# Reordering the stretch behind the rounds, and splitting GpSimd's two gathers around its sum

## The chip, the core and the metric

The kernel runs on one core of one Trainium2 chip. The metric is device time of that core in microseconds (us). Engines are named as the profile names them: PE (TensorE, matrix products), ACT (ScalarE), DVE (VectorE), POOL (GpSimd), SP (SyncE, here only a queue that starts DMAs). Each engine runs its own list of instructions in order; they wait for one another by semaphores.

## What is computed

16384 tokens (rows of 512 numbers) pass through a layer norm, then two branches whose product is added to the input. One branch is a circular filter in the Fourier domain followed by a small error-correcting code; the other is a mixture of 8 experts, of which each token uses two.

```
xn = _layernorm(x, axis=-1)
# branch s
x1  = ifft(fft(xn) * filt).real
bits = (sigmoid(x1 @ W_el + b_el) > 0.5)
s = x1 + golay_correct(bits) @ W_le + b_le
# branch g
logits = xn @ router_w.T
probs = softmax(logits); topk_vals, topk_idx = top_k(probs, 2)
expert_out = einsum('nh,eho->eno', xn, expert_weights)
g = silu(sum over the two experts of (expert_out + prob) * weight)
x = x + s * g
```

## The kernel before

Four stages follow one another. Times are from the profiled execution.

**Rounds (0 to 233 us).** Eight rounds of 16 tiles of 128 tokens each read all tokens, compute logits and bits, and store a 32-number information row per token in DRAM (`token_info`). Every token gets a slot in a table sorted by its pair of experts (`pair_tokens`).

**The stretch behind the rounds (233 to 283 us).** Two things happen side by side. First, the table is turned into a list of tiles: DVE computes where the last round's tokens go, and makes 16 pairs of marks (L1208, L1209) that PE multiplies (L1459); DVE copies the product (L1225); PE multiplies it and two loaded rows with a selection matrix (L1465); DVE writes the token list `tile_tok` (L1227); ACT copies its columns to `gidx` (L727); POOL gathers by them (L560 token rows `x2`, L562 information rows `inf2`). Second, the experts' weights are split into two fp16 parts: `high` on ACT (L646 sum half, L647 difference half) writes the high part `w_hi`; the low part `w_lo` of the first `ON_PE` = 4 experts in `EXPERT_ORDER` is made by PE, four chunks each (L1450, L1451), and evicted by ACT (L710); that of the other four by DVE in the next stage (`low_sums` L966, `low_differences` L973, each 128x1024, at the steps in `LOW_AT`).

**Extra tiles (283 to 373 us).** 27 tiles (n = 1 to 27; tile 0 is a placeholder) that hold tokens of two neighbouring pairs, one expert each. For tile n: gather (POOL), `halves_of` (DVE, L1264 to L1268), `high_part` (ACT, L733), `low_part` (DVE, L1274), a turn by eight PE transposes (L1492), its copy (ACT, L758), twelve matmuls (PE, L1481 to L1483), scaling (ACT, L775), adding (DVE, L1286). `extra_step(n)` on PE turns tile n+1 before it multiplies tile n; on DVE it does `halves_of(n+4)`, `low_part(n+3)`, the addition of n, and then the expert work of `LOW_AT`.

**Main tiles (373 to 1208 us).** 128 tiles, in loops over four. For each tile PE does 24 expert matmuls (L1481 to L1483) and 13 of the filter (L1523 to L1531). POOL adds the input (`step`, L582: sg2 + x2), then gathers tile m+4 into the same buffers (L560, L562), then scatters the finished tile (L566). `gidx` for tile m+4 is copied by ACT as the last act of its own step m (L727). A tile's buffers are taken as landed when both gathers have counted on the one semaphore `ld_x2[k]`. SP turns a tile by a DMA transpose (L459) once DVE's split and ACT's bits are there.

The order of the work on each engine is the order in which it is written; no scheduler moves it.

## Time and profile before

| | us |
|---|---|
| median of three runs | 1216.6 (1215.72 to 1217.47) |
| the profiled execution, its own time | 1215.48 |
| its span, first to last instruction | 1213.6 |
| rounds | 233 |
| stretch behind the rounds | 50.4 |
| extra tiles, 27 | 90 |
| main tiles, 128 | 835 |

The stage borders are read from the first expert matmul (283.43) and the last of the extra tiles (about 373). A line of the timeline gives start, duration, engine, line and operation, then in brackets how long the engine sat idle before it and what released it.

### The profile page before, as it was taken

The page shows a single profiled execution, that of the slowest core. Times are in us where ns is not written, and L with a number is a line of the kernel's source. Part 1 is how long each engine was busy: PE and PEld are TensorE (multiplying, and loading weights), DVE is VectorE, ACT ScalarE, POOL GpSimd, SP SyncE. Part 2 cuts the span into 40 slices and gives each one's busy share as a digit, 9 for nine tenths or more (in the row PEclk, how much of TensorE's full clock was granted, in tenths as well). Part 3 has the DMA queues.
Part 4 walks back from the last instruction along what each step waited for, and adds up shares of the span by engine and source line. Part 5 has one row for each costly group of instructions (what it writes and reads, how often), then busy time and mean ns, then how long its engine had stood idle before and what let it go on. Part 6 is the DMA issues. An engine that isn't in the chain of part 4 may idle for free. (4 is left out here: it accounts for less than half of the span.)

```text
span 1213.6 us, 27062 instructions
## 1 busy us (share of the span) xinstructions
PE 1138.5 (94%) x6310; PEld 613.3 (51%) x6311; DVE 1039.4 (86%) x2368; ACT 641.5 (53%) x1531; POOL 811.2 (67%) x715
## 2 busy tenths in 40 slices
PE   5999898667999999999999999999999999999996
PEld 4555555333454455554555555555555555555553
DVE  6799999977886889899888888888888888888874
ACT  4466656466784434434555545554555455555543
POOL 1226656846783777777777777777777777777774
PEclk9999999878999999999999999999999999999998
DMA  8656756013555776667455455555545554554552
GB/s 324 228 202 219 222 177 182 18 34 103 166 170 150 169 173 172 158 177 164 120 129 137 121 127 138 128 129 129 136 122 132 133 127 130 129 132 125 130 134 76
DMA packets 205774, 178.17 MB, mean 147 GB/s; under 512 B 164671, under 2 KB 171247, under 8 KB 201634
## 3 DMA queue, kind: packets, MB, share of 16 engines
q1 hardware_dynamic: 170258, 98.61, 32.1%
q0 software_dynamic: 31248, 76.95, 21.7%
q10 hardware_dynamic: 4224, 2.10, 0.6%
q8 instruction: 19, 0.31, 0.1%
q14 instruction: 25, 0.20, 0.0%
HBM read 94.83 MB, written 45.02 MB: 115 GB/s over the span
## 5 line engine op out<-in xcount | busy, mean ns | idle before, releaser
L1481 PE MATMUL banks<-w_hi,arena 128*128 (+1 forms) x1076 | 409.1, 380 | 6.0 <-DMA arena<-arena 4.3
L1483 PE MATMUL banks<-w_hi,arena 128*128 (+1 forms) x1076 | 408.7, 380 | 0.0
L1482 PE MATMUL banks<-w_lo,arena 128*128 (+1 forms) x1076 | 408.7, 380 | 0.0
L560 POOL DMA_INDIRECT xbuf<-in_L_attn_x,gidx x155 | 175.9, 1135 | 139.9 <-POOL xbuf L582 88.8
L733 ACT ACTIVATE arena<-xbuf,inf 128x512 f16<-128x512 f32 x141 | 101.8, 722 | 279.8 <-DVE xbuf L1268 279.8
L562 POOL DMA_INDIRECT inf<-token_info,gidx x155 | 192.9, 1245 | 52.3 <-issue 51.0
L582 POOL TENSOR_TENSOR xbuf<-xbuf 128x512 f32<-128x512 f32 x128 | 167.2, 1306 | 39.8 <-DVE xbuf L1325 34.3
L1264 DVE TENSOR_TENSOR xbuf<-xbuf 128x256 f32<-128x256 f32 x155 | 148.4, 957 | 50.8 <-DMA inf<-token_info,gidx 43.9
L531 POOL DMA_INDIRECT pair_tokens<-tok,slot x112 | 110.9, 990 | 98.1 <-DVE slot L1107 65.8
L1481 PEld LDWEIGHTS banks<-w_hi,arena 128*128 128x128 f16 x1076 | 105.3, 98 | 128.6 <-issue 16.6
L566 POOL DMA_INDIRECT out<-xbuf,sidx x128 | 142.7, 1115 | 41.3 <-issue 40.7
L1483 PEld LDWEIGHTS banks<-w_hi,arena 128*128 128x128 f16 x1076 | 105.4, 98 | 124.6 <-issue 1.0
L1482 PEld LDWEIGHTS banks<-w_lo,arena 128*128 128x128 f16 x1076 | 105.3, 98 | 111.9 <-issue 0.8
L1308 DVE SCALAR_TENSOR_TENSOR arena<-banks,cab,xT 128x512 f32<-128x512 f32 x128 | 95.9, 749 | 31.9 <-PE banks L1483 28.3
L1402 PE MATMUL banks<-xT,wcat 128*128 128x512 f32 x256 | 120.6, 616 | 0.8 <-issue 0.4
L1274 DVE SCALAR_TENSOR_TENSOR arena<-xbuf,inf,arena 128x512 f16<-128x512 f32 x141 | 105.8, 750 | 11.7 <-ACT arena L733 8.1
L1325 DVE TENSOR_TENSOR xbuf<-xbuf,arena 128x512 f32<-128x512 f32 x128 | 88.7, 693 | 17.4 <-DVE xbuf L1319 0.5
L1319 DVE TENSOR_TENSOR xbuf<-xbuf 128x256 f32<-128x256 f32 x256 | 97.4, 422 | 4.4
L752 ACT ACTIVATE cab<-inf,unscale 128x1 f32 x256 | 73.9, 288 | 42.9 <-issue 42.1
L789 ACT ACTIVATE xbuf<-banks 128x384 f32<-128x384 f32 x128 | 62.3, 487 | 63.9 <-PE banks L1531 63.7
L1265 DVE TENSOR_TENSOR xbuf<-xbuf 128x256 f32<-128x256 f32 x155 | 95.4, 615 | 0.0
L793 ACT ACTIVATE arena<-arena,inf 128x512 f32<-128x512 f32 x128 | 91.1, 712 | 2.7 <-DVE arena L1308 2.7
(322 smaller groups left out, 1877.2 us busy)
## 6 DMA issues: line engine op xcount, KB each, us to landing
xbuf<-in_L_attn_x SPq DMA_DIRECT2D x32, 1024.0 KB, 6.0
arena<-in_L_ffn_expert_weights SPq DMA_DIRECT2D x8, 1024.0 KB, 9.6
arena<-extra_sums SPq DMA_DIRECT2D x30, 256.0 KB, 2.7
extra_sums<-arena SPq DMA_DIRECT2D x28, 256.0 KB, 2.5
xbuf<-in_L_attn_x,gidx POOLq DMA_INDIRECT x155
inf<-token_info,gidx POOLq DMA_INDIRECT x155
token_info<-info ACTq DMA_DIRECT2D x8, 256.0 KB, 5.9
arena<-arena SPq DMA_TRANSPOSE x128
```

Source lines behind the costliest of these rows:

```text
L531: pool.indirect_dma_start(out=pair_slots, out_offset=bass.IndirectOffsetOnAxis(ap=slot[:, buf, t:t + 1], axis=0), in_=tok[:, buf, t:t + 1] ...
L560: pool.indirect_dma_start(out=x2[:, k], out_offset=None, in_=x_rows, in_offset=tokens, bounds_check=N - 1, oob_is_err=False).then_inc(ld_x ...
L562: pool.indirect_dma_start(out=inf2[:, k], out_offset=None, in_=info_dram, in_offset=tokens, bounds_check=N - 1, oob_is_err=False).then_inc ...
L566: pool.indirect_dma_start(out=out_rows, out_offset=bass.IndirectOffsetOnAxis(ap=sidx[:, k:k + 1], axis=0), in_=o2[:, k % 2], in_offset=Non ...
L582: G.tensor_tensor(o2[:, b], sg2[:, b], x2[:, k], ALU.add).then_inc(o_ready, 1)
L733: nc.scalar.activation(hi4[ring(i, k)], uv2[:, b], ACT.Copy, scale=inf2[:, k, 1:2]).then_inc(hi_ready, 1)
L1264: V.tensor_tensor(raw2[:, b, 0:H], x2[:, k, 0:H], x2[:, k, H:E], ALU.add).then_inc(raw_ready, 1)
L1274: V.scalar_tensor_tensor(lo4[ring(i, k)], uv2[:, b], inf2[:, k, 1:2], hi4[ring(i, k)], ALU.mult, ALU.subtract).then_inc(split_ready, 1)
L1402: last = mm(psum[:, 2], wcat[:, c], xT4[:, k % 2, c], start=(c == 0), stop=(c == C - 1))
L1481: mm(ps, hi[:, c], wh, start=(c == 0), stop=False)
L1482: mm(ps, hi[:, c], wl, start=False, stop=False)
L1483: end = mm(ps, lo[:, c], wh, start=False, stop=(c == C - 1))
```

## The change

**The low parts.** `ON_PE` goes from 4 to 3: the fourth expert's low part goes from PE and ACT to DVE. Its sum half stands in front of DVE's wait for the token list, its difference half and the fifth expert's sum half in front of the first `halves_of`. The remaining halves are spread by `SUMS_AT` and `DIFFERENCES_AT` over steps 1, 2, 3, 13 and 19, where `LOW_AT` had both halves together at 1, 2, 3 and 12.

**ACT's order.** `high` is cut in halves, and one eviction (`low_chunk`) stands before each of eight of them. Two evictions of the third expert's low part come ahead of `gidx`, two behind.

**PE's order.** Two chunks of the third expert stand between the marks and the selection product, two behind it.

**DVE's order.** Eleven small operations that stood behind the 16 pairs of marks are put among the first six pairs (`tile_places`).

**POOL's step.** In the main tiles the information row's gather for tile m+4 comes ahead of the sum of tile m, behind new waits for `gidx_ready` and `g_ready` (ACT has read the buffer's last value for tile m), and the token rows' gather stays behind the sum.

```diff
-    LOW_AT = {1: 4, 2: 5, 3: 6, 12: 7}
-    ON_PE = 4
+    ON_PE = 3
+    SUMS_AT = {2: 5, 3: 6, 13: 7}
+    DIFFERENCES_AT = {1: 4, 2: 5, 3: 6, 19: 7}
...
+                if not last:
+                    pool.wait_ge(gidx_ready, j + U + 1)
+                    pool.wait_ge(g_ready, m + 1)
+                    pool.sem_inc(g_seen, 1)
+                    gather_info(k)
                 pool.wait_ge(sg_ready, m + 1)
...
-                if not last:
-                    pool.wait_ge(gidx_ready, j + U + 1)
                 pool.wait_ge(o_ready, m + 1)
                 pool.sem_inc(o_seen, 1)
                 if not last:
-                    gather(k)
+                    gather_rows(k)
                 scatter_out(k)
...
-            for n in range(3):
-                high(EXPERT_ORDER[n])
-            low(0)
-            high(EXPERT_ORDER[3])
-            low(1)
-            for n in range(4, NE - 1):
-                high(EXPERT_ORDER[n])
+            high(EXPERT_ORDER[0])
+            high(EXPERT_ORDER[1])
+            for n in range(2):
                 for c in range(C):
+                    low_chunk(n, c)
+                    high_half(EXPERT_ORDER[2 + 2 * n + c // 2], c % 2)
+            high(EXPERT_ORDER[6])
+            low_chunk(2, 0)
+            low_chunk(2, 1)
...
-            low(2)
-            low(3)
             high(EXPERT_ORDER[NE - 1])
+            low_chunk(2, 2)
+            low_chunk(2, 3)
...
             V.tensor_copy(tokTl, psum[:, 0, 0:P]).then_inc(rows_float, 1)
+            low_sums(3)
             dve.wait_ge(toks_mm, 1)
...
             dve.sem_inc(split_ready, 1)
+            low_differences(3)
+            low_sums(4)
             halves_of(0, 1)
...
-                if n in LOW_AT:
-                    low_parts(LOW_AT[n])
+                if n in SUMS_AT:
+                    low_sums(SUMS_AT[n])
+                if n in DIFFERENCES_AT:
+                    low_differences(DIFFERENCES_AT[n])
...
             last.then_inc(last_mm, 1)
-
+            low(2, (0, 1))
...
-            low(2)
-            low(3)
+            low(2, (2, 3))
```

PE in the stretch behind the rounds, before: the marks' product, the selection product, then all of the third expert (the fourth, eight more such rows, follows it). `arena` and `w_lo` hold the weights' halves, `latT` the rows that are selected.

```order
L1459 MATMUL banks<-arena 128x128 [waits last_marks] x16
L1465 MATMUL banks<-latT 128x156 [waits rows_float]
L1465 MATMUL banks<-latT 128x156 x2
L1450 MATMUL banks<-w_lo,arena 128x512 [waits low_out,scaled_ready,whi_ready]
L1451 MATMUL banks<-w_hi,minus_h 128x512
L1450 MATMUL banks<-w_lo,arena 128x512 [waits low_out]
```

PE at the same place, after:

```order
L1493 MATMUL banks<-arena 128x128 [waits last_marks] x16
L1484 MATMUL banks<-w_lo,arena 128x512 [waits low_out,scaled_ready,whi_ready]
L1485 MATMUL banks<-w_hi,minus_h 128x512
L1484 MATMUL banks<-w_lo,arena 128x512 [waits low_out]
L1485 MATMUL banks<-w_hi,minus_h 128x512
L1499 MATMUL banks<-latT 128x156 [waits rows_float]
L1499 MATMUL banks<-latT 128x156 x2
```

Two chunks, four rows, have moved ahead of the selection product.

ACT at the end of the same stretch, before: the token indices, then eight evictions, then the last expert's high part, then the first extra tile.

```order
L727 ACTIVATE gidx<-tile_tok 128x1 [waits tiles_ready]
L727 ACTIVATE gidx<-tile_tok 128x1 x3
L710 ACTIVATE w_lo<-banks 128x512 [waits low_mm] x8
L646 ACTIVATE w_hi<-w_lo,wscale 128x1024
L647 ACTIVATE w_hi<-arena,wscale 128x1024
L733 ACTIVATE arena<-xbuf,inf 128x512 [waits uv_ready,live_ready,pad_ready]
```

ACT at the same place, after:

```order
L727 ACTIVATE w_lo<-banks 128x512 [waits low_mm] x2
L746 ACTIVATE gidx<-tile_tok 128x1 [waits tiles_ready]
L746 ACTIVATE gidx<-tile_tok 128x1 x3
L660 ACTIVATE w_hi<-w_lo,wscale 128x1024
L662 ACTIVATE w_hi<-arena,wscale 128x1024
L727 ACTIVATE w_lo<-banks 128x512 [waits low_mm] x2
L752 ACTIVATE arena<-xbuf,inf 128x512 [waits uv_ready,live_ready,pad_ready]
```

Six of the eight evictions behind the indices are gone from there: two stand ahead of them, four (the fourth expert's) are no longer made.

POOL in one main step of the loop, before: the sum, the two gathers, the scatter.

```order
L581 ISA [waits sg_ready]
L582 TENSOR_TENSOR xbuf<-xbuf 128x512 [waits stored0]
L585 REGISTER_ALU [waits sidx_ready]
L560 DMA xbuf<-in_L_attn_x,gidx 128x512 [waits gidx_ready,o_ready]
L562 DMA inf<-token_info,gidx 128x32
L566 DMA out<-xbuf,sidx 16384x512
```

POOL in the same step, after:

```order
L591 REGISTER_ALU [waits gidx_ready]
L568 DMA inf<-token_info,gidx 128x32 [waits g_ready]
L596 ISA [waits sg_ready]
L597 TENSOR_TENSOR xbuf<-xbuf 128x512 [waits stored0]
L562 DMA xbuf<-in_L_attn_x,gidx 128x512 [waits sidx_ready,o_ready]
L572 DMA out<-xbuf,sidx 16384x512
```

The information gather and the wait for `gidx_ready` have moved ahead of the sum; a wait for `g_ready` is new.

## Rows read from the trace of the kernel before

**Rows 1.** Timeline (start, us, operation) of PE's weight loads: first filter matmul, neighbouring main tiles.

```profile
1002.42 0.10 PEld L1523 LDWEIGHTS banks<-wle,arena 96*128 96x128 bf16 x1
...
1008.81 0.10 PEld L1523 LDWEIGHTS banks<-wle,arena 96*128 96x128 bf16 x1
```

**Rows 2.** The same instruction by line: count, ns min/median/max, first and last start.

```profile
L1523 PE MATMUL banks<-wle,arena x128: 381/381/382, 380.3 to 1202.0; 96*128 96x512 bf16 x128
```

**Rows 3.** Timeline of PE among the extra tiles: turns that waited (idle before, releaser).

```profile
304.16 0.62 PE L1492 MATMUL banks<-ident_h,xT 128*128 128x128 f16 x8 [1.77 <-DVE xT L1274]
333.46 0.62 PE L1492 MATMUL banks<-ident_h,arena 128*128 128x128 f16 x8 [1.75 <-DVE arena L1274]
```

**Rows 4.** Timeline of PE, stretch behind the rounds.

```profile
264.56 1.93 PE L1465 MATMUL banks<-latT 128*128 128x156 f32 x6 [2.15 <-DVE latT L1225]
266.28 1.91 PE L1450 MATMUL banks<-w_lo,arena 128*128 128x512 f32 x2
...
275.88 1.02 PE L1450 MATMUL banks<-arena 128*128 128x512 f32 x2
...
283.43 0.61 PE L1481 MATMUL banks<-w_hi,arena 128*128 128x512 f16 x1 [0.22 <-ACT arena L758]
```

**Rows 5.** Timeline of POOL, the same stretch: token rows of tiles 1 and 2.

```profile
268.30 1.02 POOL L560 DMA_INDIRECT xbuf<-in_L_attn_x,gidx  x1 [10.57 <-ACT gidx L727]
...
270.92 1.00 POOL L560 DMA_INDIRECT xbuf<-in_L_attn_x,gidx  x1 [0.30 <-issue]
```

**Rows 6.** Timeline of DVE, the same stretch.

```profile
262.02 0.19 DVE L1211 TENSOR_REDUCE spots<-tq 128x1 f32<-128x28 f32 x1
...
263.88 0.42 DVE L1223 TENSOR_TENSOR latT<-tokT,latT 128x256 f32<-128x256 int32 x1
...
266.52 0.32 DVE L1227 TENSOR_SCALAR tile_tok<-banks 128x156 int32<-128x156 f32 x1 [2.02 <-PE banks L1465]
...
272.33 0.43 DVE L1264 TENSOR_TENSOR xbuf<-xbuf 128x256 f32<-128x256 f32 x1 [3.02 <-DMA inf<-token_info,gidx]
...
280.47 0.75 DVE L1274 SCALAR_TENSOR_TENSOR arena<-xbuf,inf,arena 128x512 f16<-128x512 f32 x1 [1.88 <-ACT arena L733]
```

**Rows 7.** Timeline of ACT, the same stretch.

```profile
267.18 0.47 ACT L727 ACTIVATE gidx<-tile_tok 128x1 int32<-128x1 int32 x4
...
277.65 1.14 ACT L646 ACTIVATE w_hi<-w_lo,wscale 128x1024 f16<-128x1024 f32 x1
...
279.73 0.71 ACT L733 ACTIVATE arena<-xbuf,inf 128x512 f16<-128x512 f32 x1
```

**Rows 8.** Timeline of DVE among the extra tiles: one half of an expert's low part.

```profile
294.72 1.28 DVE L966 SCALAR_TENSOR_TENSOR w_lo<-w_lo,wscale,w_hi 128x1024 f16<-128x1024 f32 x1
```

**Rows 9.** The page's groups of POOL: busy us, mean ns of one, idle before.

```profile
L560 POOL DMA_INDIRECT xbuf<-in_L_attn_x,gidx x155 | 175.9, 1135 | 139.9 <-POOL xbuf L582 88.8
...
L562 POOL DMA_INDIRECT inf<-token_info,gidx x155 | 192.9, 1245 | 52.3 <-issue 51.0
L582 POOL TENSOR_TENSOR xbuf<-xbuf 128x512 f32<-128x512 f32 x128 | 167.2, 1306 | 39.8 <-DVE xbuf L1325 34.3
...
L566 POOL DMA_INDIRECT out<-xbuf,sidx x128 | 142.7, 1115 | 41.3 <-issue 40.7
```

**Rows 10.** Timeline of POOL over a main tile's sum and the next gather.

```profile
704.03 1.27 POOL L582 TENSOR_TENSOR xbuf<-xbuf 128x512 f32<-128x512 f32 x1
706.17 1.13 POOL L560 DMA_INDIRECT xbuf<-in_L_attn_x,gidx  x1 [0.87 <-POOL xbuf L582]
```

**Rows 11.** Timeline of DVE over the same main tile.

```profile
703.24 0.69 DVE L1325 TENSOR_TENSOR xbuf<-xbuf,arena 128x512 f32<-128x512 f32 x1
704.12 1.48 DVE L1264 TENSOR_TENSOR xbuf<-xbuf 128x256 f32<-128x256 f32 x1 [0.19 <-DMA inf<-token_info,gidx]
```

**Rows 12.** Timeline of ACT over the same main tile.

```profile
703.31 0.18 ACT L727 ACTIVATE gidx<-tile_tok 128x1 int32 x1
...
707.68 0.49 ACT L789 ACTIVATE xbuf<-banks 128x384 f32<-128x384 f32 x1 [0.44 <-PE banks L1531]
```

More of the change, by code:

```diff
@@ L322, in build @@
         o_seen = sem("o_seen")
+        g_seen = sem("g_seen")
         last_marks, last_mm = sems("last_marks last_mm")
@@ L554, in _, with gather_rows @@
                 pool.wait_ge(info_stored[b], 16 * (R // 2))
-            def gather(k):
+            def gather_rows(k):
                 tokens = bass.IndirectOffsetOnAxis(ap=gidx[:, k:k + 1], axis=0)
@@ L568, in scatter_out, with gather @@
                                         bounds_check=N - 1, oob_is_err=False).then_inc(stored[k % 2], 16)
+            def gather(k):
+                gather_rows(k)
+                gather_info(k)
             def extra_gather(n):
@@ L588, in step @@
                 if not last:
-                    gather(k)
+                    gather_rows(k)
                 scatter_out(k)
@@ L642, in _, with high_half @@
             norm(1)
+            def high_half(e, part):
+                if part == 0:
+                    nc.scalar.activation(w_hi[:, e, 0:CH], quart[:, e], ACT.Copy, scale=wscale[:, e, 1:2])
+                else:
+                    nc.scalar.activation(w_hi[:, e, CH:C], diff[:, DIFF_AT[e]], ACT.Copy, scale=wscale[:, e, 0:1]).then_inc(whi_ready, 1)
             def high(e):
-                nc.scalar.activation(w_hi[:, e, 0:CH], quart[:, e], ACT.Copy, scale=wscale[:, e, 1:2])
-                nc.scalar.activation(w_hi[:, e, CH:C], diff[:, DIFF_AT[e]], ACT.Copy, scale=wscale[:, e, 0:1]).then_inc(whi_ready, 1)
+                high_half(e, 0)
+                high_half(e, 1)
             def latT_copy(i, k):
@@ L704, in _, with low_chunk @@
             act.wait_ge(wsc_ready, 1)
-            def low(n):
-                e = EXPERT_ORDER[n]
-                for c in range(C):
-                    act.wait_ge(low_mm, C * n + c + 1)
-                    nc.scalar.activation(w_lo[:, e, c], psum[:, LOW_BANKS[c]], ACT.Copy).then_inc(low_out, 1)
-            for n in range(3):
-                high(EXPERT_ORDER[n])
-            low(0)
-            high(EXPERT_ORDER[3])
-            low(1)
-            for n in range(4, NE - 1):
-                high(EXPERT_ORDER[n])
+            def low_chunk(n, c):
+                act.wait_ge(low_mm, C * n + c + 1)
+                nc.scalar.activation(w_lo[:, EXPERT_ORDER[n], c], psum[:, LOW_BANKS[c]], ACT.Copy).then_inc(low_out, 1)
+            high(EXPERT_ORDER[0])
+            high(EXPERT_ORDER[1])
+            for n in range(2):
+                for c in range(C):
+                    low_chunk(n, c)
[3 more added lines that the diff above has]
+            low_chunk(2, 1)
             def bits_part(i, k):
@@ L974, in low_differences @@
                                        ALU.subtract).then_inc(wlo_ready, 1)
-            def low_parts(n):
-                low_sums(n)
-                low_differences(n)
             def stat(i, k, q):
@@ L1206, in _, with note, tile_places @@
             link(V.scalar_tensor_tensor(tokTf[:, 1], iota_c, tsel[:, 1, 1:2], tokTf[:, 1], ALU.is_ge, ALU.mult))
+            def note(ins):
+                n[0] += 1
+                ins.then_inc(dch, 1)
+            def tile_places(t):
+                if 0 < t < 6:
+                    dve.wait_ge(dch, n[0])
+                if t == 0:
+                    V.tensor_reduce(upto_n, up_to, AXX, ALU.add)
+                    V.tensor_reduce(shared, to_tile[:, 0, 0:NX], AXX, ALU.max)
+                    note(V.tensor_tensor_scan(home, carry_c[:, 1:NQ * TB:TB], opens, -1.0, ALU.mult, ALU.add))
+                if t == 1:
+                    V.tensor_tensor(homes, home, own_c, ALU.mult)
+                    note(V.scalar_tensor_tensor(apart, lane_c, 1.0, home[:, NQ - 1:NQ], ALU.add, ALU.add))
+                if t == 2:
+                    V.tensor_reduce(own_home, homes, AXX, ALU.add)
+                    note(V.tensor_tensor(apart, apart, upto_n, ALU.subtract))
+                if t == 3:
+                    note(V.scalar_tensor_tensor(gap, upto_n, 1.0, apart, ALU.subtract, ALU.subtract))
+                if t == 4:
+                    V.tensor_scalar(to_tile[:, 1, NX:NT], iota_c, own_home, None, ALU.is_equal)
+                    note(V.scalar_tensor_tensor(spot, gap, shared, apart, ALU.mult, ALU.add))
+                if t == 5:
+                    V.tensor_scalar(to_tile[:, 0, NX:NT], iota_c, spot, None, ALU.is_equal)
             for t in range(TB):
@@ L1210, in _ @@
                                 ALU.mult).then_inc(last_marks, 1)
[L1211 to L1221 removed]
+                tile_places(t)
             dve.wait_ge(rows_loaded, 32)
@@ L1440, in _, with low @@
             rank(R - 1)
-            def low(n):
+            def low(n, chunks=range(C)):
                 e = EXPERT_ORDER[n]
@@ L1446, in low @@
                 pe.wait_ge(scaled_ready, 2 * n + 2)
-                for c in range(C):
+                for c in chunks:
                     after(pe, low_out, C * (n - 1) + c + 1)
```

14 lines of the change are left out of this document (3 added, 11 removed).

## The prediction

> **What bounds the kernel now.** I read PE's pace in the main tiles first, then the turns that waited among the extra tiles, then the timelines of all engines in the stretch behind the rounds.
>
> The main tiles are set by PE. Where nothing waits, a tile's first filter matmul stands 6.39 us behind that of the tile before [rows 1]; over all 128 tiles the mean is (1202.0 - 380.3) / 127 = 6.47 [rows 2]. All that PE loses there is 0.08 x 127 = 10 us of 822, and no edit of the main step can give back more. The extra tiles are near PE's pace too, but for three turns that waited 1.75 to 1.77 us each for DVE's split; the last two are in [rows 3], the first lies five microseconds ahead of them. In the stretch behind the rounds PE has done its last weight chunk at 277 and starts the first extra tile at 283.43 [rows 4]. That is a chain over all engines, and there time is to be had.
>
> What ends that chain? Tile 1's rows are requested at 268.30 [rows 5] and DVE halves them from 272.33 [rows 6] to about 273.6. But ACT converts them only at 279.73, straight behind the last expert's high part that began at 277.65 [rows 7]: it had eight evictions to get through, paced by PE's low parts of two experts. Not the gather is late, but ACT's queue.
>
> **Part 1, the start of the extra tiles.** Four evictions and one expert on PE are gone, two more evictions are ahead of the indices. Behind the indices ACT has the last high part (2.1 us, 277.65 to 279.73, [rows 7]) and two evictions (together one us, half as wide as a conversion of 1.04). Even with indices at 270 it is free by 273.7, before tile 1 is halved. So the gather is late next. From the first request G (268.30 before): tile 2's rows are requested 2.62 later [rows 5]; a tile's halves start 4.03 behind its request (268.30 to 272.33, [rows 5, 6]), tile 2's at G + 6.65. They count because DVE halves tiles 1 and 2 before it splits tile 1. They take 1.2, so the split starts at G + 7.85. From there to the first expert matmul it is 283.43 - 280.47 = 2.96 [rows 4, 6]. The first extra tile starts at G + 10.8. With G unchanged: 279.1, a gain of 4.3.
>
> **Part 2, what moves G.** DVE's small operations took 1.86 us (262.02 to 263.88, [rows 6]), in part waiting for each other. Among the marks they cost about 1.2 (an estimate from these rows: a third of the time is links). PE's selection product could start half a microsecond earlier than 264.56 [rows 4], if PE were free. It isn't: two chunks now stand ahead of it. A chunk's two fp32 matmuls took 1.91 us at 266.28, at the half clock, and 1.02 at 275.88, at the full one [rows 4]; with the third matmul two chunks are 4.2 or 2.15. They start behind the last mark, at about 263.6.
> - At the full clock the chunks end at 265.8 and the product (1.2 instead of 1.93) at 267.0. ACT reached the indices at 267.18, straight from a conversion [rows 7], and now has two evictions more ahead of them, so the indices come at 268.2, 1.0 later.
> - At the half clock the chunks end at 267.8, the product at 269.7, and the indices come at 270.1, 2.9 later.
>
> PE's rate came back while it worked without a break between these two rows, and the chunks give it such work earlier. I take the middle: chunks until 267.4, the product at the full rate, indices at 269.2, 2.0 later. G is then 270.3, the first extra tile starts at 281.1, a gain of **2.3 us**, with ends of 1.4 and 3.3. POOL has two scalings fewer and waits for the indices in every case (10.57 us before, [rows 5]): nothing.
>
> DVE has new work there, three halves of 1.28 us [rows 8]. The first lies in its wait for the selection product (2.02, [rows 6], longer now), the other two in the wait for tile 1's rows (3.02, [rows 6]): nothing, at worst 0.5.
>
> **Part 3, low parts among the extra tiles.** Before, DVE has eight halves of 1.28 there [rows 8], two each in steps 1, 2, 3 and 12. Now it has seven: one in step 1, two each in 2 and 3, one in 13 and one in 19. The two waits near 299 and 304 (3.5 together) follow steps 1 to 3. One half less takes up to 1.28 off, but DVE's first addition comes some 0.4 later against PE's start than before, as DVE waits for tile 2; I take 0.8. The wait at 333.46 (1.75, [rows 3]) follows two halves in one step; with one half it should lose 1.28, less a little for step 19. I take 1.2. Sum: **2.0 us**, ends 0.8 and, with all three waits gone, 5.3.
>
> **Part 4, POOL's main step.** POOL works nearly as long per tile as PE: 1.14 + 1.25 + 1.31 + 1.12 [rows 9], a gap of 0.87 [rows 10] and two of 0.3 make 6.3 us against 6.39 to 6.47. The reorder leaves this sum and adds a wait and a count. What does it do to the landing? Before, the information rows are requested last, 1.43 behind the token rows (1.13 and 0.3). Now the token rows are last and nothing comes between sum and request. Against that the sum is later. The product is ready at 703.24 + 0.69 = 703.93 [rows 11], and the sum followed at 704.03 [rows 10]. The indices that the gather needs are written at 703.49 [rows 12] and it takes 1.0 to 1.3, so the sum starts at about 704.85, 0.8 later. And the token rows (256 KB against 16) take some 0.7 longer to land, an estimate from the 4.03 for both and the 1.3 between their requests. So 1.43 earlier, 0.8 and 0.7 later: about zero. What the later sum touches has little room: ACT idles 0.44 before its next eviction [rows 12], DVE 0.19 before its halves [rows 11]. Queued behind the new wait on POOL are the sum, the scatter and tile m+4's token rows. I take **0**, ends of 3 us each way: of the 10 us that PE loses, the waits for transposed tiles are the part that a landing could change.
>
> DVE's first halving takes 1.48 us beside POOL's sum [rows 11], and 0.43 where POOL sums nothing [rows 6]. The Trainium skill (SBUF — State Buffer, Who interferes with whom) says that a DVE instruction with two SBUF inputs and a GpSimd instruction that reads SBUF exclude each other, for the whole of the one that came first. By this rule the later sum blocks one of the next three operations for as long, and nothing is won; by the row alone one could hope for 1 us of DVE time per tile, which isn't late anyway. The sum of the terms is the same by both.
>
> **Sum.** 2.3 + 2.0 + 0 = 4.3 us. The profiled execution took 1215.48; with 4.3 off it is 1211.2. It lies 1.1 below the median of 1216.6, so the median comes to **1212.3 us**.
>
> **Rivals.** First, the start barely moves and the turns go on waiting: PE stays at the half clock and the indices come 2.9 later (1.4 gained), DVE gives 0.8, the main tiles cost 0.5. 1214.9, no change. For it: pairs of 1.91 us at this very place. Against: ACT's queue falls away in any case.
>
> Second, POOL's step becomes the pace of the main tiles. A circle closes over two tiles: indices of tile m, gather (1.3), sum (1.3), gap (0.9), landing of the token rows (3.4, from 4.03 less 0.6), halves beside the sum (2.3), ACT's conversion, eviction, activation, bits, two coefficients and the next indices (about 3.5). That is 12.7 us, and PE does two tiles in 12.8 to 12.9. It decides once the circle grows by 0.2. At 0.1 us per tile beyond PE's pace it costs 12 us in 120 tiles: 1216.6 - 4.3 + 12 = 1224. For it: DVE already waited for the information rows [rows 11], and the later sum uses up what room there is. Against: POOL's own work is no longer.
>
> Third, the landing is earlier and helps: PE's waits in the main tiles fall by 3, and all three turns among the extra tiles are in time (5.3). With 2.3 at the start that is 10.6, 1206.0.
>
> Fourth, the edits of the stretch don't do what they say: DVE's three halves delay tile 1, or the indices wait for ACT, and the first matmul stays at 283. Part 3 alone is left: 1214.6, no change.
>
> **Chances.** Forecast 0.52 (1209 to 1214); first and fourth together 0.2; second 0.13; third 0.15. The range of 8 in 10 runs from 1206.0 to 1218.0: the third case to the first and fourth with the worst end of Part 4; it leaves out most of the second. What a measurement of this kernel can tell from no change is about 0.2%, 2.4 us; faster means below 1214.2. From the cases: faster 0.67, same 0.2, slower 0.13.
>
> **What would show it.** The first expert matmul at 281 (279.8 to 282.2) instead of 283.43, with ACT idle before tile 1's conversion and DVE waiting for tile 2's rows: Part 1. The index copy at about 269, behind the selection product and not behind ACT's conversions: Part 2; the time of the two chunks shows the clock. Shorter waits of the turns and none near step 12: Part 3. The filter's matmuls 6.47 apart on average: Part 4; 6.5 or more is the second rival, with POOL never idle or waiting for the indices. The forecast is wrong if the first matmul comes earlier but the end of the extra tiles does not, or if the spacing moves either way by more than 0.03.

## The result and the profile after

The changed kernel takes 1281.49 us, median of four runs (1278.05 to 1284.93), against 1216.16 for the kernel before, run beside it (four runs, 1214.67 to 1217.47). The ratio is 1.0538, 95% interval 1.0512 to 1.0563: 65 us slower, where 4 us faster was forecast. The span of the profiled execution is 1279.0.

**Where the time went.** The filter's first matmul by line, the instruction of [rows 2] (count, ns, first and last start):

```profile
L1556 PE MATMUL banks<-wle,arena x128: 381/381/382, 378.8 to 1267.8; 96*128 96x512 bf16 x128
```

Up to the first main tile the changed kernel is 1.5 us ahead (378.8 against 380.3). Then a tile takes (1267.8 - 378.8) / 127 = 7.00 us instead of 6.47; this mean distance is called the spacing in what follows. That is 0.53 x 127 = 67 us: the whole loss lies in the main tiles. It runs through all of them, but not evenly. By PE's weight load for this matmul, the first 32 tiles take 7.25 us each (378.62 to 610.60; before 6.57), the other 95 take 6.92 (before 6.44).

**Who is waited for.** The page's groups of after, columns as in [rows 9]:

```profile
L1514 PE MATMUL banks<-w_hi,arena 128*128 (+1 forms) x1076 | 411.5, 382 | 57.4 <-DMA arena<-arena 53.9
...
L752 ACT ACTIVATE arena<-xbuf,inf 128x512 f16<-128x512 f32 x141 | 101.8, 722 | 447.5 <-DVE xbuf L1298 447.5
L568 POOL DMA_INDIRECT inf<-token_info,gidx x155 | 172.8, 1115 | 165.4 <-ACT gidx L746 82.4
L562 POOL DMA_INDIRECT xbuf<-in_L_attn_x,gidx x155 | 171.2, 1105 | 144.2 <-issue 125.5
...
L1294 DVE TENSOR_TENSOR xbuf<-xbuf 128x256 f32<-128x256 f32 x155 | 137.2, 885 | 55.7 <-DMA xbuf<-in_L_attn_x,gidx 38.3
```

Every engine waits: PE for the transposed tile, ACT for DVE's halves, DVE for the token rows, and POOL, ahead of its information gather, for ACT's indices. None is busy all the time: POOL's busy time even fell to 786.2 us (811.2 before). Each waits for the next one, and the last for the first. That is a closed chain: a circle of waits in which no single engine's load sets the pace.

**The closed chain, followed once round.** Timelines of the changed kernel over two main tiles (start, duration, engine, line; idle before in brackets). In POOL's step for tile m the rows of tile m+4 are requested; DVE and ACT halve and convert them in their step m+2, where ACT also copies the index of tile m+6, and POOL's step m+2 waits for that index. So one round of the circle spans two tiles. POOL:

```profile
702.87 1.01 POOL L562 DMA_INDIRECT xbuf<-in_L_attn_x,gidx  x1 [0.87 <-issue]
...
706.11 1.02 POOL L568 DMA_INDIRECT inf<-token_info,gidx  x1 [0.90 <-ACT gidx L746]
707.16 1.27 POOL L597 TENSOR_TENSOR xbuf<-xbuf 128x512 f32<-128x512 f32 x1
709.30 1.11 POOL L562 DMA_INDIRECT xbuf<-in_L_attn_x,gidx  x1 [0.87 <-issue]
...
713.33 1.18 POOL L568 DMA_INDIRECT inf<-token_info,gidx  x1 [1.17 <-DVE xbuf L1355]
714.54 1.27 POOL L597 TENSOR_TENSOR xbuf<-xbuf 128x512 f32<-128x512 f32 x1
716.68 1.02 POOL L562 DMA_INDIRECT xbuf<-in_L_attn_x,gidx  x1 [0.87 <-issue]
```

DVE and ACT in the same stretch:

```profile
705.23 0.69 DVE L1355 TENSOR_TENSOR xbuf<-xbuf,arena 128x512 f32<-128x512 f32 x1
706.48 2.24 DVE L1294 TENSOR_TENSOR xbuf<-xbuf 128x256 f32<-128x256 f32 x1 [0.56 <-DMA xbuf<-in_L_attn_x,gidx]
...
709.24 0.28 DVE L1298 TENSOR_TENSOR xbuf<-xbuf 128x128 f32<-128x128 f32 x1
```

```profile
705.00 0.18 ACT L746 ACTIVATE gidx<-tile_tok 128x1 int32 x1
...
709.64 0.72 ACT L752 ACTIVATE arena<-xbuf,inf 128x512 f16<-128x512 f32 x1 [3.46 <-DVE xbuf L1298]
...
710.64 0.71 ACT L812 ACTIVATE arena<-arena,inf 128x512 f32<-128x512 f32 x1
...
712.20 0.20 ACT L746 ACTIVATE gidx<-tile_tok 128x1 int32 x1
```

Token rows are requested at 702.87 and halved from 706.48 (3.61). The halves end at 709.52 and ACT converts at 709.64 (3.16). ACT's eviction, activation, bits, coefficients and index copies end at 712.40 (2.76). The information gather starts at 713.33 (0.93), the sum at 714.54 (1.21), and the token rows two tiles further on are requested at 716.68 (2.14). Together that is 13.81 us for two tiles, 6.91 a tile, and PE's own pace is 6.39 [rows 1].

The profile puts POOL's wait at 713.33 down to DVE's line 1355, the product, which had ended at 713.28. But the gather has no wait for the product, only for the index and for ACT's activation (`gidx_ready`, `g_ready`). At 706.11 it stands 0.93 behind the index copy's end (705.18), and at 713.33 again 0.93 (712.40). It was the index both times, and not in these two tiles alone: between 600 and 1150 us the gather starts 0.91 to 0.99 behind the end of an index copy in 78 of 80 tiles. DVE waits for token rows in 40 of the 80, nearly every second one. The code makes two such circles, one tile apart; in the tiles between, DVE comes to the halves straight from its own work (at 713.20 without a wait), so the circle with the waits sets the pace. The mean round over that stretch, from one request of token rows to the second one behind it, is 13.83 us.

In the kernel before, the indices were ready at 703.49 and the gather that needed them started at 706.17 [rows 10, 12], 2.68 later. With the 0.93 off, ACT had 1.7 us to spare there. The change puts the sum and its gap (2.14) and a gather (1.2) between the indices and the token rows' request, all on one path.

**The start of the extra tiles** came as forecast in this execution. PE's rows of the changed kernel that answer to [rows 4], and ACT's and POOL's to [rows 7] and [rows 5]:

```profile
262.62 1.22 PE L1484 MATMUL banks<-w_lo,arena 128*128 128x512 f32 x2
264.07 1.91 PE L1484 MATMUL banks<-w_lo,arena 128*128 128x512 f32 x2
266.20 1.29 PE L1499 MATMUL banks<-latT 128*128 128x156 f32 x6
...
280.80 0.61 PE L1514 MATMUL banks<-w_hi,arena 128*128 128x512 f16 x1 [0.24 <-ACT arena L777]
```

```profile
267.97 0.48 ACT L746 ACTIVATE gidx<-tile_tok 128x1 int32<-128x1 int32 x4 [0.73 <-DVE tile_tok L1257]
```

```profile
269.11 1.02 POOL L562 DMA_INDIRECT xbuf<-in_L_attn_x,gidx  x1 [13.49 <-ACT gidx L746]
```

### The profile page after: what moved, and what is told of

It reads as the page before. It is cut to its first block and busy times, and to the rows that moved or that the text cites. A ratio compares the mean times of both kernels' runs of the same rounds, so it can differ in the third digit from the quotient of the medians.

```text
span 1279.0 us, 27154 instructions
## 1 busy us (share of the span) xinstructions
PE 1148.3 (90%) x6298; PEld 610.2 (48%) x6299; DVE 1119.8 (88%) x2370; ACT 626.7 (49%) x1527; POOL 786.2 (61%) x713
## 5 line engine op out<-in xcount | busy, mean ns | idle before, releaser
L568 POOL DMA_INDIRECT inf<-token_info,gidx x155 | 172.8, 1115 | 165.4 <-ACT gidx L746 82.4
L562 POOL DMA_INDIRECT xbuf<-in_L_attn_x,gidx x155 | 171.2, 1105 | 144.2 <-issue 125.5
L1294 DVE TENSOR_TENSOR xbuf<-xbuf 128x256 f32<-128x256 f32 x155 | 137.2, 885 | 55.7 <-DMA xbuf<-in_L_attn_x,gidx 38.3
L572 POOL DMA_INDIRECT out<-xbuf,sidx x128 | 148.0, 1156 | 41.3 <-issue 40.1
L597 POOL TENSOR_TENSOR xbuf<-xbuf 128x512 f32<-128x512 f32 x128 | 162.8, 1272 | 13.7 <-DVE xbuf L1355 10.4
L533 POOL DMA_INDIRECT pair_tokens<-tok,slot x112 | 110.9, 990 | 97.7 <-DVE slot L1121 65.5
L1297 DVE SCALAR_TENSOR_TENSOR xbuf<-xbuf,inf 128x128 f32<-128x128 f32 x155 | 133.7, 863 | 0.0
L1295 DVE TENSOR_TENSOR xbuf<-xbuf 128x256 f32<-128x256 f32 x155 | 115.8, 747 | 0.0
L1349 DVE TENSOR_TENSOR xbuf<-xbuf 128x256 f32<-128x256 f32 x256 | 98.3, 425 | 4.4
```

The lines of the kernel that those rows point to most:

```text
L533: pool.indirect_dma_start(out=pair_slots, out_offset=bass.IndirectOffsetOnAxis(ap=slot[:, buf, t:t + 1], axis=0), in_=tok[:, buf, t:t + 1] ...
L562: pool.indirect_dma_start(out=x2[:, k], out_offset=None, in_=x_rows, in_offset=tokens, bounds_check=N - 1, oob_is_err=False).then_inc(ld_x ...
L568: pool.indirect_dma_start(out=inf2[:, k], out_offset=None, in_=info_dram, in_offset=tokens, bounds_check=N - 1, oob_is_err=False).then_inc ...
L572: pool.indirect_dma_start(out=out_rows, out_offset=bass.IndirectOffsetOnAxis(ap=sidx[:, k:k + 1], axis=0), in_=o2[:, k % 2], in_offset=Non ...
L597: G.tensor_tensor(o2[:, b], sg2[:, b], x2[:, k], ALU.add).then_inc(o_ready, 1)
L1294: V.tensor_tensor(raw2[:, b, 0:H], x2[:, k, 0:H], x2[:, k, H:E], ALU.add).then_inc(raw_ready, 1)
```

## The experiments

Three explanations were tried against each other, called C, P and L. **C**: the early wait for the indices closes a chain over two tiles. **P**: DVE's two-input operations are held up beside POOL's sum (2.24 us in the row above, 1.48 in [rows 11]); DVE loses that time, and it sets the pace. **L**: the sum, and the token rows behind it, are late, however that comes about.

Beside e1 to e4 the kernel before took 1292.03 us (median of 19 runs), beside e5 to e12 it took 1216.4 to 1216.6. e1 and e12 are the same kernel: in e1 the main tiles begin some 60 us later and take 0.07 us more each. The cause isn't known; e1 to e4 and e9 to e12 are on record under the same chip number. So only ratios to the kernel before, run beside each, and spacings of one group are compared. The spacing comes from one execution, the ratio from all. No kernel leaves out any part of the computation.

### e1: the edits of the stretch alone

```diff
-                if not last:
-                    pool.wait_ge(gidx_ready, j + U + 1)
-                    pool.wait_ge(g_ready, m + 1)
-                    pool.sem_inc(g_seen, 1)
-                    gather_info(k)
...
+                if not last:
+                    pool.wait_ge(gidx_ready, j + U + 1)
...
-                    gather_rows(k)
+                    gather(k)
```

(against the changed kernel)

> The changed kernel with POOL's main step put back as it was before (sum, both gathers, scatter); all edits of the stretch and of the extra tiles stay. If the whole loss comes from POOL's step, the filter's matmuls are 6.47 us apart again and the first of them stays at 378.8 instead of 380.3: 1216.2 - 1.5 = about 1214.7. If the edits of the stretch harm the main tiles too, it stays above 1220.

Measured: 1287.01 us, ratio 0.9971 (0.9938 to 1.0004), spacing 6.54. The loss is gone with the step. The times that were expected for e1 and e2 were those of the other group; the ratios answer them.

### e2: POOL's new step alone

The kernel before with the new step, and nothing of the stretch.

```diff
+                if not last:
+                    pool.wait_ge(gidx_ready, j + U + 1)
+                    pool.wait_ge(g_ready, m + 1)
+                    pool.sem_inc(g_seen, 1)
+                    gather_info(k)
...
-                if not last:
-                    pool.wait_ge(gidx_ready, j + U + 1)
...
-                    gather(k)
+                    gather_rows(k)
```

> The kernel before with only POOL's main step changed (information gather ahead of the sum, token gather behind it). If the two parts of the change are independent: 1216.2 + 67 = about 1283, the filter's matmuls 7.0 us apart. If the loss needs the stretch's edits too: near 1216.

Measured: 1347.71 us, ratio 1.0441 (1.0403 to 1.0480), spacing 6.98. The step alone does the harm: 0.044 of 1292 is 57 us, 0.45 a tile, and the spacing is 0.44 over e1's. The kernel with the closed chain keeps its spacing in both groups (6.98 here, 7.00 for the changed kernel), while e1's is 0.07 over e12's, so the ratio is smaller here than 1.0538.

### e3: POOL drained between gather and sum

The changed kernel; behind the information gather POOL also writes one element per partition and waits for that write.

```diff
+                    G.memset(drain[:, :], 0.0).then_inc(drained, 1)
+                    pool.wait_ge(drained, m + 1)
                 pool.wait_ge(sg_ready, m + 1)
```

> The changed kernel; between the information gather and the sum POOL also writes one element per partition and waits for that write, so the sum is handed out only when the gather's own work on POOL is over. Theory P (the sum handed out behind the gather keeps DVE's two-input operations out from about 0.55 us after the gather's start, 0.6 us longer than the sum lasts): the blocked DVE operation falls from 2.1 to about 1.5 us, and the time falls by 25 us or more, to 1255 or less. Theory L (only the lateness of the sum counts, since token rows land later): the sum comes some 0.2 us later still, so the time stays at 1281 or grows by up to 10.

Measured: 1341.57 us, ratio 1.0394 (1.0358 to 1.0430), spacing 6.98. The changed kernel itself has no run in this group, so e2, with the same step, stands for it. Windows of e2 and then of e3, 600 to 1150 (us; PE, weight loads, DVE, ACT, POOL, each busy us and count; clock, DMA share, GB/s):

```profile
600.00:1150.00 550.00, 518.78 (x2944) 267.53 (x2943) 494.81 (x883) 253.31 (x711) 362.34 (x319) 1.00 0.55 125
```

```profile
600.00:1150.00 550.00, 514.70 (x2923) 266.15 (x2923) 405.30 (x875) 255.23 (x708) 375.14 (x395) 1.00 0.51 123
```

DVE's busy time falls by 89.5 us of 550, to 74% of the window, and the tiles come no faster: P falls. L had forecast no gain, and stands so far. The block, the time for which DVE's operation is held, shrank, but the landing, the time from a request to the first use, grew, as e3's rows show:

```profile
905.20 1.26 POOL L601 TENSOR_TENSOR xbuf<-xbuf 128x512 f32<-128x512 f32 x1
...
907.33 1.02 POOL L564 DMA_INDIRECT xbuf<-in_L_attn_x,gidx  x1 [0.87 <-issue]
```

```profile
911.67 1.41 DVE L1298 TENSOR_TENSOR xbuf<-xbuf 128x256 f32<-128x256 f32 x1 [2.64 <-DMA xbuf<-in_L_attn_x,gidx]
```

From the request to the halves it is 4.34 us here and 3.61 in the changed kernel. Over 600 to 1150, where DVE waits for token rows, the median is 4.40 (38 waits) against 3.56 (40). Two tiles take 2 x 6.98 = 14.0 us in e2 and in e3, made up differently.

### e4: a late sum without the early gather

The kernel before, with one more wait ahead of the sum, for the scaled product of the next tile's first expert. The index wait stays behind the sum.

```diff
+                if not (last and k + 1 >= U):
+                    pool.wait_ge(t_ready, m + 2)
```

> The kernel before with the sum of tile m also waiting for the first expert's scaled product of tile m+1, an event 0.75 to 0.9 us behind the product it adds; the order of POOL's work is untouched and nothing stands between. Theory L (a sum that is late by itself, through the landing of the rows gathered behind it, sets the pace): rows land 0.8 later, so 0.2 to 0.4 us per tile, 1240 to 1265. Theory P: the sum alone blocks DVE for 1.5 us as before and lateness of this size is taken up: below 1225.

Measured: 1291.48 us, ratio 1.0018 (0.9992 to 1.0043), spacing 6.59. The cost that L forecast does not come. But the lateness came out smaller than the 0.8 us that was expected: between 600 and 1150 the sum starts on average 0.75 behind the product, against 0.21 in e1, and 1.34 in the changed kernel. So e4 shows that half a microsecond of lateness costs at most 0.4%. By itself it doesn't rule out L at the changed kernel's size; e5 goes further.

### e5: the index copies one place earlier

In the changed kernel ACT copies the indices behind the bits and ahead of the two coefficients.

```diff
-                    main_coef(*at(i, k, 2))
...
+                if not (last and k + 2 >= U):
+                    main_coef(*at(i, k, 2))
```

> The changed kernel; ACT copies the two indices ahead of its two coefficients instead of behind them, 0.6 us earlier. Theory C (a circle over two tiles sets the pace: indices ready, 0.93 to the gather's start, 1.05 gather, 2.14 from the sum's start to the token rows' request, 3.6 to 3.9 to their halving, 3.0 for the halves, 2.9 to the next indices, together 13.9): the circle loses 0.6, each tile 0.3 us, 128 tiles 38 us: 3% less than the changed kernel, a ratio to before of 1.02. Theory P (DVE's time lost to the long block): the gather still lies in front of the sum and the block stays 2.1 us: ratio 1.04 or more.

Measured: 1242.60 us, ratio 1.0201 (1.0173 to 1.0228), spacing 6.69. Six tenths of the loss go when two small ACT operations change places: 0.31 us a tile, as C forecast (0.3). In e5 the sum stands on average 0.83 behind the product, hardly more than in e4 (0.75), yet a tile takes 0.22 more than before, where e4's takes 0.05 more than e1's. So it isn't lateness alone that costs. DVE is still blocked as long in such a tile:

```profile
905.53 2.07 DVE L1296 TENSOR_TENSOR xbuf<-xbuf 128x256 f32<-128x256 f32 x1
```

### e6: the index one tile ahead

In the changed kernel ACT copies, in step m, the index of tile m+5 in place of m+4.

```diff
-        tile_tok = sb("tile_tok", [P, NT], I32)
+        tile_tok = sb("tile_tok", [P, NT + 1], I32)
...
-                    gather_index(i + 1, k)
+                    gather_index(i + 1 + (k + 1) // U, (k + 1) % U)
...
+            gather_index(XR + 1, 0)
```

> The changed kernel; ACT copies the gather index one tile ahead (for tile m+5 in its step m), so POOL's early gather waits only for ACT's activation of tile m, 1.07 us earlier than the index was. Theory C: the circle is 12.8 or less, within PE's 12.8 to 12.9 for two tiles; the pace is PE's again: ratio to before 0.99 to 1.005. Theory P: the product comes 0.9 us after the gather's start, so the block shrinks to about 1.5 as well, and it would recover too; but then DVE's blocked operation must be seen to be short. If both are wrong: 1.04.

Measured: 1213.42 us, ratio 0.9973 (0.9957 to 0.9989). By line:

```profile
L1558 PE MATMUL banks<-wle,arena x128: 381/381/382, 380.2 to 1201.0; 96*128 96x512 bf16 x128
```

The spacing is (1201.0 - 380.2) / 127 = 6.46: the whole loss is gone. The information gather is still ahead of the sum. It starts 0.85 behind the end of ACT's activation that frees its buffer, and waits for no index (the next index copy is at 906.92, behind it). The sum follows 0.33 behind the product (907.56), and DVE is still held, for 1.63 us. POOL, ACT and DVE of e6:

```profile
906.84 1.02 POOL L568 DMA_INDIRECT inf<-token_info,gidx  x1 [0.75 <-issue]
907.89 1.27 POOL L597 TENSOR_TENSOR xbuf<-xbuf 128x512 f32<-128x512 f32 x1
```

```profile
905.28 0.71 ACT L812 ACTIVATE arena<-arena,inf 128x512 f32<-128x512 f32 x1
...
906.92 0.19 ACT L746 ACTIVATE gidx<-tile_tok 128x1 int32 x1
```

```profile
906.83 0.73 DVE L1357 TENSOR_TENSOR xbuf<-xbuf,arena 128x512 f32<-128x512 f32 x1
...
907.82 1.63 DVE L1297 TENSOR_TENSOR xbuf<-xbuf 128x256 f32<-128x256 f32 x1
```

With e6 the circle through the index spans three tiles; its 14 us are then 4.7 a tile. A circle over two tiles is left, through the activation, for which the gather waits too. It is shorter by what ACT does between the activation and the end of the index copy, 1.05 us in the rows of the changed kernel (711.35 to 712.40), so some 12.8 us (an estimate from 13.81), and PE sets the pace again. That is close: there is little room left. C is shown: between this kernel and the changed one, only the tile whose index is copied has changed. That the block is shorter too (1.63) can't be the reason, since e3 shortened it and gained nothing.

### e7 and e8: the gathers behind the sum, in other orders

e7 is the kernel before with the order sum, token rows, scatter, information rows. e8 is the changed kernel with the order sum, information rows, token rows, scatter. The first edit is e7's against the kernel before, the second e8's against the changed one.

```diff
-                    gather(k)
+                    gather_rows(k)
                 scatter_out(k)
+                if not last:
+                    gather_info(k)
```

```diff
-                if not last:
-                    pool.wait_ge(gidx_ready, j + U + 1)
-                    pool.wait_ge(g_ready, m + 1)
-                    pool.sem_inc(g_seen, 1)
-                    gather_info(k)
...
+                if not last:
+                    pool.wait_ge(gidx_ready, j + U + 1)
...
+                    gather_info(k)
                     gather_rows(k)
                 scatter_out(k)
```

> The kernel before with POOL's main step in the order sum, token rows, scatter, information rows; no wait is added or moved. Theory C for the old order (sum to sum over two tiles 12.77, of which 6.3 from the sum's start to the information rows' landing): they land 1.3 to 1.4 later, the circle is 14.1, 7.05 us per tile: ratio 1.055 to 1.06. If only the early wait and the gather in front of the sum matter: 1.00.

> The changed kernel with all of POOL's gathers behind the sum again, but the information rows first and the token rows second, then the scatter. Nothing stands in front of the sum. Theory C: the token rows are requested 1.3 later than in the old order's place for them and take 3.6 instead of 2.7 to land, so the last landing is 0.7 to 0.9 later than before: circle 13.5, 6.7 to 6.8 per tile, ratio 1.03 to 1.05. If the order of the two gathers costs nothing by itself: 0.997, as with the old step.

Measured: e7 1270.81 us, ratio 1.0427 (1.0397 to 1.0458), spacing 6.91; e8 1249.82 us, ratio 1.0290 (1.0256 to 1.0324), spacing 6.68. (e8's five runs lie between 1238.55 and 1254.59, and the trace is of the fastest.) DVE's wait ahead of its halves, first e7's and then e8's (600 to 1150; total, times, longest):

```profile
DVE xbuf L1274 <- DMA inf<-token_info,gidx: 124.3, 68, 3.7
```

```profile
DVE xbuf L1292 <- DMA xbuf<-in_L_attn_x,gidx: 84.3, 72, 3.8
```

C's forecasts were 1.055 to 1.06 for e7, which stays below it, and 1.03 to 1.05 for e8, which lies at its lower edge. No index is waited for here, and both lose. So the kernel before must have a circle too, from the sum over the landing back to the product and the sum; that one is argued from these two runs and was not followed row by row. Of the orders tried, that of before (token rows 0.87 behind the sum, information rows 1.43 behind those) is the only one in which both land early enough, as long as the indices are copied where they were. In e7 the last request is 4.9 to 5.3 us behind the sum's start instead of 3.6, and that costs 0.44 a tile. In e8 the token rows are requested 3.5 behind it instead of 2.1, and that costs 0.21 by the trace, 0.26 by the median time. So lateness does cost, if it is more than the circle has to spare: 1.3 to 1.7 us did, e4's half a microsecond didn't.

### e9 to e12: what the parts are worth

These put together the edits shown above. e9 is e1 with e6's index; e10 is e6 with the low parts spread further; e11 is the kernel before with the new step and e6's index, without the stretch; e12 repeats e1. All ran on one chip, together with 35 runs of the kernel before.

```diff
-    SUMS_AT = {2: 5, 3: 6, 13: 7}
-    DIFFERENCES_AT = {1: 4, 2: 5, 3: 6, 19: 7}
+    SUMS_AT = {2: 5, 4: 6, 13: 7}
+    DIFFERENCES_AT = {1: 4, 3: 5, 5: 6, 19: 7}
```

(e10 against e6)

> The edits of the stretch, POOL's main step as before, and the index copied one tile ahead. The old step's circle runs through the product and not through the index, so the index copy adds nothing: the same as the stretch's edits alone, ratio 0.997 to 0.999. If the split gathers are worth something once the index is early, this one is slower than e6_index_tile_ahead (0.9973) by more than 2 us; if not, the two agree.

> e6_index_tile_ahead with the extra tiles' low parts spread one half per step (sums of the fifth and sixth low part in steps 2 and 4, differences in 3 and 5, where both halves stood in 2 and in 3). The two turns that waited 1.76 us each near 298 and 303 lose 1 to 2.5 us together: ratio 0.995 to 0.997. If DVE's total and not its bunching sets these waits: 0.997 to 0.998, as e6.

> The kernel before with POOL's new step and the index copied one tile ahead, and none of the edits of the stretch. If the new step with an early index is free but gives nothing: 0.999 to 1.001. If the step gives the gain of e6_index_tile_ahead: 0.997.

> The stretch's edits alone again (as e1_stretch_only), on the same chip as the three others and in five rounds. By the traces so far the first filter matmul comes 1 to 3 us earlier than before and the main tiles' pace is the same: ratio 0.997 to 0.999, 1.2 to 3.6 us.

| kernel | stretch | POOL's step | index ahead | us | ratio (95%) | spacing |
|---|---|---|---|---|---|---|
| before | old | old | no | 1216.62 | 1 | 6.47 |
| e12 | new | old | no | 1213.72 | 0.9977 (0.9955 to 0.9998) | 6.47 |
| e9 | new | old | yes | 1214.28 | 0.9984 (0.9962 to 1.0005) | 6.46 |
| e11 | old | new | yes | 1216.06 | 1.0003 (0.9983 to 1.0023) | 6.47 |
| e10 | new, spread | new | yes | 1212.40 | 0.9968 (0.9951 to 0.9986) | 6.46 |

The stretch is worth 0.23%, 2.9 us. The split gathers, once their chain is open, are worth nothing that can be told from noise (e11: 0.2% either way), and so is the earlier index (e9). e10 is 0.3% faster than the kernel before and some 5% faster than the changed one; whether it beats e12 or e6 can't be told from these intervals.

## Why the prediction was wrong

**What bounds the kernel.** Right for the kernel before. It held for the changed one only as long as no chain between engines took longer than PE.

**Part 1 and Part 2, the start: right in mechanism; the size is met in the forecast's own execution.** The first expert matmul started at 280.80 (forecast 281.1, a gain of 2.6 against 2.3). The selection product started at 266.20 and the indices were copied from 267.97, behind DVE's list and not behind ACT's queue (forecast 269.2). Of the two chunks the first pair took 1.22 and the second 1.91: the granted clock was 0.86 of full speed from 262 to 264, 0.50 from 264 to 266 and 0.78 from 266 to 268, so the rate fell where it was assumed to rise, and that the middle came near is luck. The first request G was at 269.11 (forecast 270.3); from there to the first matmul it took 11.7, not 10.8. Tile 1's halves started at 273.88, 4.77 behind the request and not 4.03. So two misses of 1 us cancel, and that is luck as well. From one execution to another the start moves by more than the gain: with the same edits of the stretch the first matmul came at 279.8 to 282.1 in e6, e8, e9, e10 and e12 and at 284.28 in e5, and without them at 284.42 (e7) and 284.97 (e11). So 2.6 us is the difference of two executions, not a measured worth.

**Part 3, the low parts: mis-sized, nothing or a small loss instead of 2.0.** Turns that wait among the extra tiles, of the changed kernel, beside the three of 1.75 to 1.77 of before ([rows 3] has two):

```profile
289.06 0.62 PE L1525 MATMUL banks<-ident_h,arena 128*128 128x128 f16 x8 [0.92 <-DVE arena L1304]
...
292.71 0.62 PE L1525 MATMUL banks<-ident_h,arena 128*128 128x128 f16 x8 [0.44 <-DVE arena L1304]
...
297.69 0.62 PE L1525 MATMUL banks<-ident_h,xT 128*128 128x128 f16 x8 [1.76 <-DVE xT L1304]
...
302.66 0.62 PE L1525 MATMUL banks<-ident_h,xT 128*128 128x128 f16 x8 [1.76 <-DVE xT L1304]
...
333.42 0.62 PE L1525 MATMUL banks<-ident_h,arena 128*128 128x128 f16 x8 [0.22 <-DVE arena L1304]
```

The wait near 333 fell from 1.75 to 0.22, as forecast (1.2). But PE starts 2.6 us earlier, DVE doesn't, and two new waits stand at 289 and 292. Together they are 5.10 against 5.29. Four more waits of 0.29 to 0.54 stand between 340 and 366 (before: two, 0.32 and 0.21), which makes 6.74 against 5.82: PE waited 0.9 longer for DVE, not 2.0 less. In e12, with the same edit, it is 5.26 up to 303 and 0.58 behind, 5.84 in all, as before. In e10 five turns wait 1.30 to 0.44, 3.07 together, and PE waited 1.32 for the low part itself in exchange:

```profile
289.07 0.62 PE L1527 MATMUL banks<-ident_h,arena 128*128 128x128 f16 x8 [1.30 <-DVE arena L1306]
...
305.64 0.38 PE L1516 MATMUL banks<-w_hi,xT 128*128 128x512 f16 x1 [1.32 <-DVE w_lo L993]
```

That is 4.4 against 6.8 in e6, but the first main tile then waited 2.95 us for its DMA transpose, 1.1 more than in e6 (1.81). The first filter matmul came at 378.5 there, 378.0 in e12. From the first expert matmul to the first filter matmul it is 96.9 us before, 98.0 in the changed kernel, 97.2 in e12, 98.1 in e6 and 97.7 in e10: spreading the halves moves the waits from one place to another and takes 0.4 us off e6's stage, and none of the edits made it shorter than before. Parts 1 to 3 were to bring 4.3 us; e12 measures 2.9 (0.2 to 5.5).

**Part 4, POOL's main step: this step failed.** Its sentence was "The indices that the gather needs are written at 703.49 and it takes 1.0 to 1.3, so the sum starts at about 704.85, 0.8 later". The step that failed is this one, with the zero that was drawn from it: the new wait was priced by one tile's delay and not as part of a circle. Three things were wrong with it.

First, it starts the gather with the indices. The gather starts 0.93 behind them, so the sum stood 1.24 behind the product (705.92 to 707.16) where 0.92 was worked out. (From 703.49 its own 1.0 to 1.3 give 704.5 to 704.8; the 704.85 lies just above.) The rows had that price: in [rows 5, 7] the index copies start at 267.18, one takes 0.18 [rows 12], and the gather that waited for the first starts at 268.30, 0.94 later.

Second, it asks what the later sum touches in one tile. The sum's delay was put against the landing of one tile's rows and the room of ACT and DVE beside it, and the sum of that was zero. But the indices that the sum now waits for come behind ACT's conversion of the rows that the sum before last released. A delay in a closed chain isn't absorbed, it returns in every round, so the bounds of 3 us each way had no reason under them: the term was a loss of 67 us.

Third, the second rival had this chain and gave it 0.13. Term by term, forecast and measured (702.87 to 716.68):

| | forecast | measured |
|---|---|---|
| indices to gather | 0 | 0.93 |
| gather to sum | 1.3 | 1.21 |
| sum to request | 2.2 | 2.14 |
| landing | 3.4 | 3.61 |
| halves, to ACT | 2.3 | 3.16 |
| ACT to indices | 3.5 | 2.76 |
| two tiles | 12.7 | 13.81 |

It was 12.7 against PE's 12.8 to 12.9: a chain worked out at 98% of the pace, whose terms turned out up to 0.9 us off, could lie above it as well as below. With the 0.94 of its own rows it is 13.6, 6.8 a tile, (6.8 - 6.47) x 127 = 42 us over. By the measured round it is (6.92 - 6.47) x 127 = 57, and the first 32 tiles, at 7.25 each, add 11. And the rival's price, 0.1 us a tile, came from nowhere; every 0.1 us of the chain beyond 12.9 costs 6 us of the kernel. "POOL's own work is no longer" was true and spoke against nothing: the chain has waits and landings in it, not work.

**The block beside the sum.** The prediction left open whether one operation would be held as long as before or not. It is held longer. The Trainium skill (SBUF — State Buffer, Who interferes with whom) has the two instructions exclude each other, from the start of the one that came first. At 706.48 DVE's operation came 0.68 ahead of the sum's recorded start, and it ended with the sum (708.72 against 708.43), 2.24 us instead of the 1.48 of [rows 11] or the 0.43 of an undisturbed one. By that rule, taken with the recorded starts, the sum would have waited for DVE; the row shows the reverse. Either the sum holds DVE off from before its recorded start, or the rule doesn't cover this case; no run here tells which. As time of DVE the block didn't matter (e3). The 0.8 us by which the halves exceed their forecast are part of the chain.

**The rivals.** The first, third and fourth: the start did move, the landing didn't help, the edits did what they say. The sign to watch was named ("6.5 or more is the second rival, with POOL never idle or waiting for the indices"), and it is what the profile shows.

**Still open.** Why the landing of the token rows takes 4.4 us in e3 and 3.6 in the changed kernel, and with it why e3 gained nothing from a shorter block. In most of e3's long landings POOL begins the next information gather within 2.91 us of the request (3.2 or more in most tiles of the changed kernel), but six landings of e5 with the gather at 2.90 to 2.92 took 3.60 to 3.67, so this order alone is not the cause. Open too is why the first 32 main tiles lose 0.68 us each and the others 0.48. The round of 13.83 that was read between 600 and 1150 fits the latter (2 x 6.92), and not the mean of 7.00. And why the kernel before took 1292 us beside e1 to e4.

## What to carry to other kernels

Before a wait is moved earlier on an in-order engine, follow it round: from what it waits for, back through every engine, until the chain meets the moved instruction again; divide by the number of tiles it spans, and compare that with the pace, not the engines' busy times. A chain that was worked out at 98% of the pace ran at 107% of it here (13.83 against 12.9), so one that comes this near deserves most of the forecast's doubt, and its price is its excess times all rounds. To open one, take its input from a tile earlier (e6: one index copied one step ahead took the ratio from 1.054 to 0.997) before shortening anything in it.

## What the runs showed of the hardware

- A gather on POOL that waited for ACT's index copy starts 0.93 us behind that copy's end (706.11, 713.33 in the changed kernel, 903.94 in e3; 0.91 to 0.99 in 78 of 80 tiles of the changed kernel), and one that waited for ACT's activation 0.85 behind it (906.84 in e6). Behind the end of POOL's own sum a gather starts 0.87 later (709.30, 716.68), and behind another gather 0.30 [rows 5].
- Where POOL's sum is queued right behind a gather and has its inputs, a two-input operation of DVE can be held before the sum's recorded start. In the changed kernel, between 600 and 1150, 76 of them that started up to 0.74 us ahead of it took 1.7 to 2.3 us and ended 0.15 to 0.30 behind the sum; those that started 0.76 or more ahead took their usual 0.28 to 0.43. In e3, where POOL was drained between the two, none that started ahead of the sum was held, and none took more than 1.53.
- The same kernel ran in 1287 us (e1) and in 1214 us (e12). The main tiles began at 439.5 instead of 378.0 and took 6.54 us instead of 6.47. The cause isn't known.
